# First loads of the attention asked for inside the depthwise stage, xn and k1 stored in its first half, constants cleared early

## The reference

```
k1   = conv1d over channels, 9 taps, one filter per pixel (xn) + bias
a    = softmax over 9 taps of  w2 @ relu(bn(w1 @ stack([xn, k1])))      # per image and channel
v    = depthwise 3x3 convolution (xn) + bias
out1 = sum over 9 neighbouring channels of v * a  + k1
ks   = relu(bn(depthwise 3x3 convolution (xn)))
a2   = softmax over pixels of  grouped 1x1 (relu(bn(grouped 1x1 ([ks, xn]))))
out2 = ks + a2 * xn
x    = x + alpha * out1 + (1 - alpha) * out2
```

## Time and profile before

| | us |
|---|---|
| median of 3 runs | 1621.7 (1620.54 to 1624.31) |
| the profiled execution | 1627.32 |
| its span | 1625.6 |
| TensorE busy | 1309.9 (81%) |
| VectorE busy | 1087.0 (67%) |
| ScalarE busy | 772.1 (47%) |
| GpSimd busy | 568.0 (35%) |
| mean granted clock of TensorE | 0.885 of full |

### The profile page before, as it was taken

How to read it: one execution, slowest core, us unless ns; L and a number is a source line. 1 busy time by engine, 2 the same in 40 slices (tenths; PEclk the granted TensorE clock), 3 DMA queues, 4 the chain that set the end, 5 groups by cost and what they waited for, 6 DMA issues and landing times.

```text
span 1625.6 us, 36996 instructions
## 1 busy us (share of the span) xinstructions
PE 1309.9 (81%) x9796; PEld 1078.3 (66%) x9797; DVE 1087.0 (67%) x2553; ACT 772.1 (47%) x1828; POOL 568.0 (35%) x561
## 2 busy tenths in 40 slices
PE   0196999799999999986746501999999999999692
PEld 0186999756766666666746501888888888888531
DVE  6796555357888877874566662777777777777462
ACT  0294666344445444442576771455554545555200
POOL 0162111134433444330377775233333333333200
PEclk9997999889999999995555555999999999999896
DMA  8535566778778777661144354222222222222297
GB/s 321 139 92 192 202 241 235 252 176 188 188 170 202 179 185 189 162 148 54 54 150 135 131 179 158 76 85 91 91 91 87 84 89 90 90 91 77 85 423 310
DMA packets 258517, 251.16 MB, mean 155 GB/s; under 512 B 150009, under 2 KB 234446, under 8 KB 255204
## 3 DMA queue, kind: packets, MB, share of 16 engines
q1 hardware_dynamic: 238093, 197.20, 41.1%
q0 software_dynamic: 20320, 53.45, 9.6%
q10 hardware_dynamic: 66, 0.05, 0.0%
HBM read 152.34 MB, written 105.75 MB: 159 GB/s over the span
## 4 chain that ended last, share of the span: by engine, by line
PE 59%; DVE 15%; DMA 9%; issue 5%; ACT 5%; SPq 2%; POOL 2%; DVEq 0%; ACTq 0%; POOLq 0%
PE ps L690 15%; PE ps L675 14%; PE ps L490 5%; PE ps L470 4%; DMA u_d<-in_zstrings 3%; PE ps L659 2%; DMA pool_<-y_d 2%; PE ps L542 2%; POOL rows_d L1521 2%; PE ps L515 2%; SPq L288 2%; PE ps L525 2%; DMA pool_<-in_ffn_w 2%; ACT aux L1388 2%; PE ps L459 2%
## 5 line engine op out<-in xcount | busy, mean ns | idle before, releaser
L1530 POOL DMA_INDIRECT y_d<-pool_,to_s x176 | 173.5, 986 | 361.2 <-ACT pool_ L1447 331.9
L690 PE MATMUL ps<-pool_,aux 128*128 x2112 | 248.4, 274 | 6.2 <-DVE aux L1197 3.2
L675 PE MATMUL ps<-aux,pool_ 128*128 128x256 f16 x2112 | 246.5, 274 | 0.7 <-ACT aux L1440 0.6
L690 PEld LDWEIGHTS ps<-pool_,aux 128*128 128x128 f16 x2112 | 199.7, 98 | 49.9 <-issue 25.6
L675 PEld LDWEIGHTS ps<-aux,pool_ 128*128 x2112 | 206.2, 98 | 25.9 <-issue 1.7
L1521 POOL DMA_INDIRECT rows_d<-aux,idx_s x162 | 159.2, 983 | 105.4 <-ACT aux L1390 60.0
L1440 ACT ACTIVATE aux<-ps,b_s 128x256 f32<-128x256 f32 x352 | 138.3, 475 | 93.0 <-DVE aux L1197 92.6
L1432 ACT ACTIVATE aux<-ps 128x512 f16<-128x512 f32 x88 | 52.6, 597 | 188.8 <-PE ps L659 188.8
L1515 POOL DMA_DIRECT2D pool_<-v_d x64 | 50.0, 781 | 223.5 <-PE ps L575 220.3
L1205 DVE SCALAR_TENSOR_TENSOR pool_<-ps,pool_ 128x512 f32<-128x512 f32 x88 | 60.9, 692 | 96.0 <-PE ps L690 96.0
L515 PE MATMUL ps<-pool_,se_w_s 81*81 81x512 f32 x256 | 118.8, 608 | 6.1 <-DMA pool_<-k_d 6.1
(11 more groups left out here) (204 smaller groups left out, 3030.6 us busy)
## 6 DMA issues: line engine op xcount, KB each, us to landing
pool_<-rows_d SPq DMA_DIRECT2D x88, 260.0 KB, 2.8
pool_<-y_d SPq DMA_DIRECT2D x18, 1152.0 KB, 13.9
big<-in_x SPq DMA_DIRECT2D x2, 5184.0 KB, 21.3
xn_d<-big SPq DMA_DIRECT2D x16, 648.0 KB, 3.0
v_d<-aux SPq DMA_DIRECT2D x64, 162.0 KB, 2.1
ks_d<-aux SPq DMA_DIRECT2D x64, 162.0 KB, 2.2
pool_<-xn_d SPq DMA_DIRECT2D x32, 324.0 KB
pool_<-k_d SPq DMA_DIRECT2D x32, 324.0 KB
```

The costliest lines, as they stand in the source:

```text
L675: last = nc.tensor.matmul(o, w_s[:, a, bass.ds(e * (4 * PIECE) + (k * HID + j * 128), 128)], xh_s[:, par, b, k * SLOTS:(k + 1) * SLOTS], s ...
L690: last = nc.tensor.matmul(ps[:, 6 + par, s * C:(s + 1) * C], hh_s[:, par, a, j, s * 128:(s + 1) * 128], w_s[:, b, bass.ds(e * (4 * PIECE) ...
L1530: nc.gpsimd.indirect_dma_start(out=y_d[:, :], out_offset=bass.IndirectOffsetOnAxis(ap=to_s[:, par, k:k + 1], axis=0), in_=yo_s[:, par, k, ...
```

## The change

- SP stores xn and the second half of k1 in twice as large pieces in the first 8 of its 16 turns; the second 8 turns have no such stores.
- The tiles of the attention are laid out anew in `pool_`: those filled early (`kq_s`, `xc_s`, `xr_s`, `kr_s`, `a_s`, `ap_s`) now lie over the second half of k1, behind the masks.
- After turn 12 of 16 SP waits for the stores of xn and k1, asks for the keys of groups 0 and 1, and after each of the next three turns for one kind of image tile of both groups (xn, k1, x). Only ks, for which all stores must have landed, comes after the last turn. v is asked for by GpSimd as before, which now waits for the stores itself.
- The first chunk's masks use four PSUM banks instead of two; the copy of its taps comes before the statistics, and TensorE no longer waits for `tab_c` before them.
- `ones_s` is cleared first of all, the router's matmuls and their use come before the pixel stage, `a_s` and `ap_s` are cleared before the last chunk; `t1_s` stays where it was.

```diff
--- before.py
+++ after.py
@@ -180,12 +180,9 @@
         cursor[0] = 0
-        kq_s = take(HW, 2, 2, G, C)
-        xc_s, vc_s, kc_s, xr_s, kr_s = (take(128, 2, HALVES, G, HW) for _ in range(5))
-        a_s = take(HW + 1, 2, G, C)
+        vc_s, kc_s = (take(128, 2, HALVES, G, HW) for _ in range(2))
         lg_s = take(128, G * 4, D)
         st_s = take(128, 4, G * 4)
-        ap_s = take(128, G * 4, 15)
         t1_s = take(128, G * 4, 32)
@@ -194,6 +191,12 @@
         sm_s = take(128, 2, 4, HALVES * G)
+        assert cursor[0] <= 2 * m_end
+        cursor[0] = 2 * m_end
+        kq_s = take(HW, 2, 2, G, C)
+        xc_s, xr_s, kr_s = (take(128, 2, HALVES, G, HW) for _ in range(3))
+        a_s = take(HW + 1, 2, G, C)
+        ap_s = take(128, G * 4, 15)
         cursor[0] = 0
...
@@ -307,12 +310,9 @@
             sp.wait_ge(S["xb_c"], PIX_TURNS + CREDIT)
-            with sp.Fori(0, QUADS // DEPTH) as i:
-                part = bass.ds(i * (DEPTH * QUAD * HW), DEPTH * QUAD * HW)
-                sp.dma_start(xn_d[:, part], big[:, part]).then_inc(S["xn_out"], 16)
-                part = bass.ds(i * (DEPTH * QUAD * HW // 2) + half, DEPTH * QUAD * HW // 2)
-                sp.dma_start(k1_d[:, part], pool_[:, part]).then_inc(S["k1_out1"], 16)
+            def store_quads(i):
                 for k in range(DEPTH):
@@ -321,30 +321,54 @@
                                      src[:, k]).then_inc(S[f"st_v{k}"], 16)
+            turns = QUADS // DEPTH
+            with sp.Fori(0, turns // 2) as i:
+                part = bass.ds(i * (2 * DEPTH * QUAD * HW), 2 * DEPTH * QUAD * HW)
+                sp.dma_start(xn_d[:, part], big[:, part]).then_inc(S["xn_out"], 16)
+                part = bass.ds(i * (DEPTH * QUAD * HW) + half, DEPTH * QUAD * HW)
+                sp.dma_start(k1_d[:, part], pool_[:, part]).then_inc(S["k1_out1"], 16)
+                store_quads(i)
+            with sp.Fori(turns // 2, turns - 4) as i:
+                store_quads(i)
+            def load_keys(g, par):
+                for k, src in enumerate((xn_d, k1_d)):
+                    sp.dma_start(kq_s[:, par, k], src[bass.ds(g * G, G), :]
+                                 .rearrange("b (i j) -> i b j", j=C)).then_inc(S[f"kq_in{par}"], 16)
+            def load_images(g, par, dst, src, come):
+                for h in range(HALVES):
+                    sp.dma_start(dst[:, par, h], src[bass.ds(g * G, G), h * 128 * HW:(h + 1) * 128 * HW]
+                                 .rearrange("b (c p) -> c b p", p=HW)).then_inc(S[f"{come}{par}"], 16)
+            sp.wait_ge(S["xn_out"], 16 * (turns // 2))
+            sp.wait_ge(S["k1_out0"], 16)
+            sp.wait_ge(S["k1_outm"], 16)
+            sp.wait_ge(S["k1_out1"], 16 * (turns // 2))
+            for par in range(2):
+                load_keys(par, par)
+            for k, (dst, src, come) in enumerate(((xc_s, xn_d, "c_in"), (kr_s, k1_d, "rk_in"), (xr_s, x, "rk_in"))):
+                store_quads(turns - 4 + k)
+                for par in range(2):
+                    load_images(par, par, dst, src, come)
+            store_quads(turns - 1)
             for k in range(DEPTH):
                 sp.wait_ge(S[f"st_v{k}"], 32 * (QUADS // DEPTH) + CREDIT)
-            sp.wait_ge(S["xn_out"], 16 * (QUADS // DEPTH))
-            sp.wait_ge(S["k1_out1"], 16 * (QUADS // DEPTH))
-            def load_pair(i, first=False):
+            for par in range(2):
+                load_images(par, par, kc_s, ks_d, "c_in")
+            def load_pair(i):
                 for par in range(2):
                     g = i * 2 + par
-                    rows = bass.ds(g * G, G)
-                    if not first:
-                        sp.wait_ge(S["se1_p"], 2 * g - 2)
-                    for k, src in enumerate((xn_d, k1_d)):
-                        sp.dma_start(kq_s[:, par, k],
-                                     src[rows, :].rearrange("b (i j) -> i b j", j=C)).then_inc(S[f"kq_in{par}"], 16)
-                    if not first:
-                        sp.wait_ge(S["t_c"], g - 1 + CREDIT)
+                    sp.wait_ge(S["se1_p"], 2 * g - 2)
+                    load_keys(g, par)
+                    sp.wait_ge(S["t_c"], g - 1 + CREDIT)
                     for dst, src, come in ((kc_s, ks_d, "c_in"), (xc_s, xn_d, "c_in"), (kr_s, k1_d, "rk_in"),
                                            (xr_s, x, "rk_in")):
-                        for h in range(HALVES):
-                            sp.dma_start(dst[:, par, h],
-                                         src[rows, h * 128 * HW:(h + 1) * 128 * HW]
-                                         .rearrange("b (c p) -> c b p", p=HW)).then_inc(S[f"{come}{par}"], 16)
-            load_pair(0, first=True)
+                        load_images(g, par, dst, src, come)
             with sp.Fori(1, PAIRS) as i:
@@ -412,6 +436,10 @@
             pe.wait_ge(S["w_in"], W_IN)
+            pe.wait_ge(S["ones_c"], 1)
+            for h in range(HALVES):
+                last = nc.tensor.matmul(ps[:, 6, 0:EXPERTS], ones_s[:, :], router_s[:, h, :], start=h == 0, stop=h == 1)
+            last.then_inc(S["rm_p"], 1)
             def turn_pixels(i, par):
@@ -446,17 +474,19 @@
             pe.wait_ge(S["mask_in"], 16)
-            pe.wait_ge(S["tab_c"], 1)
-            def masks(ck, groups):
+            def masks(ck, groups, banks=2):
                 if 0 in groups:
...
                     side = g % 2
-                    pe.wait_ge(S[f"mb_e{side}"], ck * (ODDS if side else EVENS) + g // 2 + CREDIT)
+                    if banks == 2:
+                        pe.wait_ge(S[f"mb_e{side}"], ck * (ODDS if side else EVENS) + g // 2 + CREDIT)
+                    elif g >= banks:
+                        pe.wait_ge(S[f"mb_e{side}"], g // 2 - 1 + CREDIT)
                     for m in range(SIZES[g]):
-                        last = nc.tensor.matmul(ps[0:HW + 1, side, m * 2 * CHUNK:(m + 1) * 2 * CHUNK]
+                        last = nc.tensor.matmul(ps[0:HW + 1, g % banks, m * 2 * CHUNK:(m + 1) * 2 * CHUNK]
                                                 .rearrange("p (v c) -> p v c", v=2),
@@ -491,19 +521,13 @@
                     last.then_inc(S["cv_p"], 1)
-            masks(0, range(len(SIZES)))
+            masks(0, range(len(SIZES)), banks=4)
             turn_quad(0, 0)
...
             convolve_chunk(CHUNKS - 1, 1, more=False)
-            pe.wait_ge(S["phase_a"], 1)
-            pe.wait_ge(S["ks_c"], QUADS + CREDIT)
-            for h in range(HALVES):
-                last = nc.tensor.matmul(ps[:, 6, 0:EXPERTS], ones_s[:, :], router_s[:, h, :], start=h == 0, stop=h == 1)
-            last.then_inc(S["rm_p"], 1)
             def keys(g, par, i, first=False):
@@ -580,6 +604,8 @@
                     keys(2 * i, 0, i, first)
+                    if first:
+                        pe.wait_ge(S["ks_c"], QUADS + CREDIT)
                 if late:
@@ -751,6 +777,7 @@
             early, unroll = 60, 15
+            nc.vector.memset(ones_s[:, :], 1.0).then_inc(S["ones_c"], 1)
             link(nc.vector.memset(taph_s, 0.0))
@@ -764,6 +791,7 @@
                     link(nc.vector.tensor_tensor(tapr_s, left, part, ALU.subtract))
+            nc.vector.tensor_copy(tapc_s[:, :, :], taph_s[:, :, 0:CHUNK]).then_inc(S["tapc_c"], 1)
             def pixel_statistics(first, pixels, run, chans, part):
@@ -795,6 +823,11 @@
             dve.wait_ge(S["w_in"], W_IN)
+            dve.wait_ge(S["rm_p"], 1)
+            for h in range(HALVES):
+                ins = nc.vector.scalar_tensor_tensor(router_s[:, h, :], ps[:, 6, 0:EXPERTS], -1.0 / C, router_s[:, h, :],
+                                                     ALU.mult, ALU.add)
+            ins.then_inc(S["rw_c"], 1)
             def transposed(i, par):
@@ -831,17 +864,16 @@
             dve.wait_ge(S["xb_c"], PIX_TURNS + CREDIT)
-            nc.vector.tensor_copy(tapc_s[:, :, :], taph_s[:, :, 0:CHUNK]).then_inc(S["tapc_c"], 1)
             nc.vector.memset(pt_s[:, :, :, :], 1.0).then_inc(S["tab_c"], 1)
             dve.wait_ge(S["tab_c"], 1)
-            def odd_masks(ck, side, groups):
+            def odd_masks(ck, side, groups, banks=2):
                 for g in groups:
...
                         nc.vector.tensor_copy(m_s[:, side, :, :, STARTS[g]:STARTS[g] + SIZES[g]].rearrange("p c v m -> p m v c"),
-                                              ps[0:HW + 1, 1, 0:SIZES[g] * 2 * CHUNK]
+                                              ps[0:HW + 1, g % banks, 0:SIZES[g] * 2 * CHUNK]
                                               .rearrange("p (m v c) -> p m v c", v=2, c=CHUNK)).then_inc(S["mb_e1"], 1)
@@ -866,28 +898,22 @@
             dve.wait_ge(S["k1_out0"], 16)
-            odd_masks(0, 0, range(len(SIZES)))
+            odd_masks(0, 0, range(len(SIZES)), banks=4)
             turned_quad(0, 0)
...
             dve_chunk(CHUNKS - 2, 0)
-            dve_chunk(CHUNKS - 1, 1, more=False)
-            dve.wait_ge(S["k1_out1"], 16 * (QUADS // DEPTH))
```

(13 more changed lines are left out.)

8 lines of the change are left out of this document (4 added, 4 removed).

## The result

The changed kernel takes 1604.55 us as median of 6 runs (1601.33 to 1614.0), the kernel before 1623.36 (6 runs): ratio 0.9896, 95% interval 0.9872 to 0.9919. Forecast were 1609 with a range of 1604 to 1616. The profiled execution took 1601.33 us, its span is 1599.6; that of before was 1627.32. So the two profiles differ by 26.0 us, 7 more than the medians (18.8), and the first thing to find out is which part of that is the change.

What follows compares the result with a forecast made beforehand. TensorE was taken to bound the full stages, leaving time only in two seams around the depthwise stage. Terms +0.3 - 3.8 + 0 + 0.1 - 9.8 = -13.2 us took the median 1621.7 to 1608.5, stated as 1609, range 1604 to 1616.

Steps and rivals of the forecast that it cites:

- the two seams: Stretches around the depthwise stage, 140.30 to 158.80 and 314.15 to 330.54, where TensorE is partly idle at clock 0.57 and 0.58.
- Term 1: Before the statistics: early copy of the first taps costs one copy and one wait more, +0.3 us (0 to +0.5).
- Term 2: First seam: four banks let ScalarE's copies follow each other, first quad at 155.0 instead of 158.79, -3.8 us (0 to -4.4).
- Term 3: Depthwise stage: doubled stores of xn and k1 in the first half delay nothing, 0 us.
- Term 4: Between chunks 6 and 7: clearing a_s and ap_s takes 2.6 us on VectorE, costing +0.1 us (0 to +1.1).
- Term 5: Second seam: early loads start the spatial matmuls at 320.7 instead of 330.54, -9.8 us (bounds -7.2 and -12.7).
- rival D: Depthwise stage: doubled bursts hold up v and ks stores, ScalarE waits for st_v in the first eight turns; 1638 us, chance 0.04.
- A: After the second seam: TensorE's clock stays low through group 1's keys, 4.7 us lost, 1614 us; chance 0.14.
- B: First seam: k1's second quarter lands at 160.8, sharing engines with larger stores; gain 1.0 for 3.8, 1612 us; chance 0.09.
- C: Second seam: kc lands after 5.3 us, 1611.5 us; chance 0.06.
- E: Attention: bound by loads rather than its own work, so the saved time isn't passed on; 1620 us, chance 0.05.

Runs made afterwards that it cites:

- each half alone: Kernel before with only four banks, early tap copy and no tab_c wait: 0.9966; changed kernel with two banks and the tab_c wait again: 0.9958.
- e_stores: Kernel before with only the stores of xn and k1 doubled in the first eight turns, none in the last eight: 1622.78 us, ratio 0.9992.
- e_loads: Changed kernel with two banks for the first masks and TensorE waiting for tab_c again: 1617.91 us, ratio 0.9958.
- e_late: Changed kernel with the first two groups' loads asked for behind the last store again: 1617.46 us, ratio 0.9947.
- e_nopool: Changed kernel without GpSimd's two passes over each group's residual (x + alpha k1 left out of the result): 1594.48 us, ratio 0.9791.
- e_warm: Changed kernel with unread matmuls added in TensorE's idle time, 34 among the first masks, 13 after the first keys: 1616.8 us, ratio 0.9921.
- e_split_again: Changed kernel with the first two groups' ks loads split, only the last 16 channels behind their landing; second execution: 1615.42 us, ratio 0.9942.
- e_scale: Changed kernel with the scaling of the residual (alpha times k1) moved from GpSimd to ScalarE: 1609.57 us, ratio 0.9913.

## Why the prediction was right

**The place of the time.** The forecast put it into the two seams and nowhere else, and that is where it is: each half alone shows its own seam changed and the other's not. By the seams the change is worth 9.2 us in the second and 5 in the first, 14 in all. The forecast's sum was 13.2. A gain of 14 us is a ratio of 0.9914, which lies within each of the three intervals measured for the changed kernel (ratios 0.9896, 0.9894 and 0.9925). The forecast was of the right size. That the number fits so far is partly luck: the medians differ by 18.8 us and not by 14, and 1604.55 is only 0.55 us above the lower end of the range. The single runs of the changed kernel scatter by up to 20 us, and its ratio on a third chip is worth 12 us.

**Term 1, early copy of the taps, +0.3.** Not visible. The last convolution over channels starts at 139.93 before and between 138.62 and 141.07 in the changed kernels, 140.05 in e_stores, which doesn't have the edit.

**Term 2, four banks, -3.8.** Mechanism as described, size too small: the chain from first copy to first quad lost 4.53 us (9.16 to 4.63), 0.7 more than worked out, and outside the term's own bound of 4.4. More comes behind it, which the sum lacked: the first convolution is 5.4 us earlier (8.31 for 13.71; 8.20 to 9.23 in the other kernels with four banks), because the clock is back when TensorE gets to it. The clock's return is what varies here: e_stores has two banks as before and 12.84, with the clock back 2.6 us after its first quad instead of 4.5. Windows of a us, of the kernel before, then of the changed one:

```profile
162.50:163.50 1.00, 1.00 (x17) 1.00 (x16) 0.69 (x1) 0.45 (x1) 0.46 (x1) 0.61 0.00 0
```

```profile
155.00:156.00 1.00, 1.00 (x6) 1.00 (x5) 0.18 (x1) 0.00 (x0) 0.00 (x0) 0.50 1.12 467
156.00:157.00 1.00, 1.00 (x11) 1.00 (x11) 0.60 (x2) 0.00 (x0) 0.46 (x1) 0.79 0.87 363
```

The clock, the third number from the end, rose at about 163 before; now TensorE is busy without a gap from 151 on and it rises between 156 and 157. And the wall that I had set at 157.9, k1's second quarter, is not there: it landed 14.2 us after 141.0, at 155.2, before VectorE asked. This store takes 15.6 us in the three kernels with two banks (before, e_loads, e_stores) and 13.5 to 14.2 in all eleven profiles with four; what the banks have to do with it is not shown.

**Term 3, doubled stores, 0.** Right. Issued beside the doubled stores (155 to 235), the v and ks stores land in 3.4 us in the median and 6.1 at most, where the forecast had 7.3 at most and 8.9 + 2.4 as the landing at which it would count. The 8.0 us of the whole stage come later, beside the first loads (stores issued in 275 to 285):

```profile
DMA to landing us min/median/max: 2.5/6.5/8.0
...
287.25 0.44 ACT L1324 ACTIVATE aux<-ps 128x324 f32<-128x324 f32 x1 [1.27 <-DMA ks_d<-aux]
```

There ScalarE did wait for a store of ks, once, 1.27 us (0.5 in the second profile, not at all in the third). The forecast had named such a wait as a sign of being wrong; it costs nothing here, the stage being 150.83 us from first to last convolution in all three. So the loads among the stores, not the doubled stores, are what comes nearest to rival D.

**Term 4, clearings before the last chunk, +0.1.** On VectorE's timeline

```profile
293.02 1.76 DVE L909 MEMSET pool_<- 82x2048 f32 x1 [0.38 <-issue]
294.90 0.26 DVE L910 MEMSET pool_<- 128x240 f32 x1
295.20 0.69 DVE L883 COPY aux<-ps 81x512 f32<-81x512 f32 x1
```

the clearings end at 295.16, the next copy follows at once, and the stage is no longer than before. Cost 0. e_late shows that taking them from the seam is worth 0.6 us at most, since they lay beside the wait for loads.

**Term 5, the second seam, -9.8.** It is -9.2. The first load was issued 3.42 us after the last convolution, where it had been 3.25, the landing was 3.2 us for the median load instead of 2.6, and TensorE started 7.17 us after the last convolution instead of 6.55. I had read the landing of a quiet moment; here four loads go out in a row, which may be why they take longer. The spatial matmuls did pass at 1.2 GHz, and the clock was back 4.7 us after their start, as the forecast had it:

```profile
318.00:319.00 1.00, 1.00 (x3) 0.59 (x3) 0.00 (x0) 0.62 (x1) 1.00 (x1) 0.50 1.02 292
...
320.20:321.20 1.00, 1.00 (x10) 1.00 (x10) 0.00 (x0) 0.98 (x2) 1.00 (x1) 0.97 0.22 55
```

**The rivals.** A (the clock stays low longer): not so in the changed kernel's three profiles; in the first the clock was low from about 313.5 (0.86 over the seam's 7.17 us is 2.0 at 1.2 GHz) to 320.2, 7 us, where it had been low for 17. But e_loads, with the same second seam, had just that: 19.55 us at 1.2 GHz from its first spatial matmul on. So A's 0.14 was no empty chance, and that none of the three profiles shows it may be luck. Falls of the clock in the middle of the attention were in no rival, and are the largest source of scatter between the profiles. B (k1's second quarter later): refuted, 155.2; it took 15.6 us both with doubled stores behind it (e_stores) and without (before). C (ks after 5.3 us): 3.2. D (stores hold the slots): refuted by e_stores. E (not passed on): refuted, each half alone has a ratio below 1 and so has the whole.

**What was missing.** The profile that the forecast started from has falls of the clock in its attention too. Its sum, made against one execution, would have been as good against any other, since the seams don't depend on them; but its range, 12 us, treats as certain that two medians of a few runs differ by the sum. The changed kernel's 19 timed runs lie between 1601.31 and 1621.27 us.

**What stays open.** Why TensorE's clock falls in the attention, in some executions at one place, in some at another, in four profiles (the changed kernel's first, e_late, e_loads, e_nopool) nowhere between the stretch behind the seam and the attention's last 24 us. In the rows it is not idle there: 11.01 of 13.70 us busy before the fall at 562.2, 13.70 of 13.70 during it. Also open are whether the split loads provoke more of these falls, what decides how long the clock stays low behind the second seam (5 us in the changed kernel, 20 in e_loads), and why the experts take 865.1 to 871.4 us.

## What to carry to other kernels

Look for the seams between stages, where the bounding engine is both idle and slow, and ask there for what the next stage reads while the stage before still runs full; what makes that possible is finishing the big stores early, and a burst cost nothing here while the small stores on the same queue landed before their slot was needed (6.1 us at most, of 11.3). Give a short serial chain of two engines (matmul, copy out) as many banks as are free: the chain fell here to ScalarE's own time (six copies in 5.73 us), and the clock came back sooner as well. Before a difference between two profiles is explained, compare stage by stage, and set the mean clock of each stage beside its length: here 11 of 26 us, and 1.3 more ahead of the seams, were not the change's.

## What the runs showed of the hardware

- TensorE's clock was at 1.2 GHz within work that kept it busy: 13.70 of 13.70 us at 0.50 (562.2 to 575.9) behind 11.01 of 13.70 busy at 1.00, and 19.55 of 19.55 in e_loads (321.15 to 340.70). In e_warm it fell in a wait of about 1.3 us right behind 7.5 us of matmuls with no gap at 1.00. The Trainium skill, TensorE: Matmul & The Clock Gate, Part 1, says that sustained busy time brings the full clock. The trace agrees for the first seam (busy from 151, back at 156.4) and does not for the stretches of 13.7 and 19.55 us.
- In the attention each us at the lower level cost 0.54 us (estimate, from the line through eleven profiles). That is about what a stage loses that TensorE bounds throughout: half the clock does half the work.
- Loads of 16 channels landed in 1.7 to 2.1 us, those of 112 channels in 4.0 to 4.1 (e_split_again), the changed kernel's of 128 in 2.6 to 3.6. What kept them late was the landing of the stores that they had to wait for (3.8 to 4.1 us instead of 2.3 to 2.5).
- VectorE's passes over 128 x 648 take 0.83 us (two tiles) and 0.89 (scalar, tensor, tensor) without GpSimd's two passes and 0.88 to 1.11 and 1.15 to 1.22 on average with them; 1.32 is the mean of the second kind in e_scale. Taking both passes away is worth 14.6 us of an attention of 418 (estimate, against the same line), of which 9.3 show directly against the best profile.
